# Gated cross-attention over 16 batches: score products in two 64-row halves of TensorE, and all orders written anew

## The reference

```python
# layer 0: full cross-attention, then a mixture of 8 experts (top 2)
x = x + tanh(g_xattn[0]) * attn0(layernorm(x), ctx)     # softmax(q k^T / sqrt(8)) v, 16 heads of 8
x = x + tanh(g_ffn[0])   * moe(layernorm(x))            # gelu(x W1 + b1) W2 + b2, top-2 router
# layer 1: cross-attention over the 32 greatest scores of each row, then self-attention + experts
scores = einsum('bhqd,bhkd->bhqk', q, k) / sqrt(8)
top_scores, top_idx = top_k(scores, 32)                 # of 1601
x = x + tanh(g_xattn[1]) * (softmax(top_scores) @ v[top_idx]) @ Wo.T
x = x + tanh(g_ffn[1])   * (self_attention(layernorm(x)) + top2_experts(layernorm(x)))
```

## Time and profile before

| | us |
|---|---|
| median of three runs | 5451.87 |
| the profiled execution, time | 5462.37 |
| the profiled execution, first to last instruction | 5460.3 |
| PE busy | 4684.1 (86%) |
| VectorE (DVE) busy | 4361.7 (80%) |
| ScalarE (ACT) busy | 4036.6 (74%) |
| GpSimd (POOL) busy | 1154.4 (21%) |
| mean granted TensorE clock | 0.936 of full |

### The profile page before, as it was taken

How to read it: one execution, slowest core, us unless ns; L and a number is a source line. 1 busy time by engine, 2 the same in 40 slices (tenths; PEclk the granted TensorE clock), 3 DMA queues, 4 the chain that set the end, 5 groups by cost and what they waited for, 6 DMA issues and landing times. The chain is left out here.

```text
span 5460.3 us, 110204 instructions
## 1 busy us (share of the span) xinstructions
PE 4684.1 (86%) x34502; PEld 2229.0 (41%) x34502; DVE 4361.7 (80%) x23240; ACT 4036.6 (74%) x5196; POOL 1154.4 (21%) x2648
## 2 busy tenths in 40 slices
PE   4878788999798889979989999997999799988776
PEld 2434334353343435334343544434353344434222
DVE  4458888878878797897879888788878888887772
ACT  1457677878687697868869788886878688787763
POOL 2121122222122222212212222222222122121110
PEclk7889899999899899989989999998999899999886
DMA  4232222223122132322313222231323223121110
GB/s 119 69 73 54 59 62 54 70 59 80 49 62 72 43 80 57 76 54 62 75 38 80 55 73 71 62 74 47 74 60 77 52 60 71 36 65 30 34 26 19
DMA packets 356337, 332.23 MB, mean 61 GB/s; under 512 B 102074, under 2 KB 313149, under 8 KB 355711
## 3 DMA queue, kind: packets, MB, share of 16 engines
q1 hardware_dynamic: 355710, 324.84, 24.3%
HBM read 217.54 MB, written 107.13 MB: 59 GB/s over the span
## 5 line engine op out<-in xcount | busy, mean ns | idle before, releaser
L942 DVE MAX8 cand<-s 128x8 f32<-128x67 f32 (+1 forms) x12288 | 1988.3, 222 | 116.8 <-ACT s L894 67.5
L913 ACT ACTIVATE prob<-wide 128x1024 f32<-128x1024 f32 (+1 forms) x1792 | 1778.7, 1025 | 390.2 <-PE wide L635 188.8
L1028 DVE TENSOR_REDUCE part<-score 128x1 f32<-128x512 f32 (+1 forms) x2048 | 1122.3, 564 | 395.4 <-PE score L594 264.1
L681 PE MATMUL att<-prob,v 128*9 128x256 f32 (+1 forms) x14336 | 1110.3, 389 | 27.9 <-ACT prob L913 26.1
L635 PE MATMUL wide<-q,k_att 128*128 128x256 bf16 (+1 forms) x6656 | 1023.4, 281 | 103.9 <-ACT s L894 56.2
L894 ACT ACTIVATE s<-wide 128x1024 f32<-128x1024 f32 (+1 forms) x1024 | 843.1, 845 | 309.6 <-DVEq L1082 174.5
L903 ACT ACTIVATE below<-wide 128x1024 bf16<-128x1024 f32 (+1 forms) x832 | 828.2, 1024 | 131.6 <-PE wide L635 123.5
L594 PE MATMUL score<-k_scan,q 128*128 128x512 bf16 (+1 forms) x2048 | 666.3, 349 | 220.9 <-DVE part L1028 178.7
L635 PEld LDWEIGHTS wide<-q,k_att 128*128 128x128 bf16 (+1 forms) x6656 | 583.3, 101 | 562.5 <-ACT s L894 149.5
L1271 POOL TENSOR_SCALAR flag<-cand,ends 128x24 bf16<-128x24 f32 x512 | 178.6, 349 | 2494.4 <-DVE ends L967 2243.5
L657 PE MATMUL wide<-below,minus_ident 128*128 128x512 bf16 (+1 forms) x1664 | 504.5, 386 | 97.2 <-ACT below L903 86.2
(11 more groups left out here) (161 smaller groups left out, 5202.2 us busy)
## 6 DMA issues: line engine op xcount, KB each, us to landing
k_scan<-k_stack SPq DMA_DIRECT2D x512, 150.1 KB, 2.6
k_stack<-split_b SPq DMA_DIRECT2D x576, 128.0 KB, 2.4
k_att<-k_stack SPq DMA_DIRECT2D x384, 192.0 KB, 3.3
ctxT<-in_ctx_dram SPq DMA_DIRECT2D x32, 800.5 KB, 5.2
q_stack<-split_b SPq DMA_DIRECT2D x192, 64.0 KB, 2.1
q<-q_stack SPq DMA_DIRECT2D x128, 96.0 KB
self_stack<-split_b SPq DMA_DIRECT2D x192, 64.0 KB, 2.1
k_self<-self_stack SPq DMA_DIRECT2D x64, 96.0 KB
```

The lines of the kernel that those rows point to most:

```text
L681: r = tensor.matmul(att[32 * j:32 * j + HD + 1, 0:S], v[0:kc, c, j0 * HG + j, :], m.prob[n % 3][0:kc, j * S:(j + 1) * S], start=(c == 0), ...
L913: scalar.activation(pr[0:kc, :], ps[0:kc, :], ACT.Exp, scale=SCALE).then_inc(sem["wide_done"], 1)
L942: i = vector.max(cand[:, :, c], s[:, KCUT[c]:KCUT[c + 1]])
L1028: vector.tensor_reduce(m.part[:, QT * hh + qt, c:c + 1], score[i % 2][:, 0:wd], AX.X, ALU.max).then_inc(sem["score_max"], 1)
```

## The change

1. The operands of the scores lie in two halves of the partitions, rows 0 to 50 and rows 64 to 114 (`UP = 64`). A product reads only one half (`tile_position=(r0, 0)`, 64 rows), and two products that follow each other read different halves and write different PSUM banks: in `n0` and `c1` two blocks of 512 keys of a head, in `s_0`, `s_1` and `s_z` two heads of the group, in `z_score` two heads.
2. `n0` now fills two banks at once, and `n0_max` takes one maximum over up to 1024 columns (1024 and 577). The two `score` banks are one buffer: PE may fill it only when the last maximum is done. `z_max` likewise covers two heads.
3. Operands are brought in for both halves: `q` twice (the same rows), `k_att` and the self-attention's in two halves, `k_scan` in three transfers (two for the upper half, one for the lower).
4. `ORDER` and `LAG` of all engines are written anew.

```diff
+UP = 64
+HALF = HG // 2
 ORDER = dict(
     pe="""
-        cut_add c1 pv.1 n0 c1 pv.1 c1 row_turn.0 c1 s_1 n0 s_1 n0 cut_add n0 cut_add w_k.1 pv.1 s_1*2 pv.1 n0*2
+        cut_add row_turn.0 cut_add s_1 pv.1 n0 s_1 pv.1 cut_add*2 flag s_1 pv.1 n0 s_1 pv.1 cut_add*2 c1 pv.1 n0 c1
...
 LAG = dict(
     pe={
-        "cut_add": 216, "c1": 244, "pv.1": 217, "n0": 255, "row_turn.0": 9, "s_1": 215, "w_k.1": 9, "flag": 62,
+        "cut_add": 217, "row_turn.0": 9, "s_1": 215, "pv.1": 217, "n0": 127, "flag": 61, "c1": 236, "row_turn.1": 16,
...
-        m.k_scan = [[sb(f"k_scan{l}_{n}", [P, NK], BF16) for n in range(2)] for l in range(2)]
-        m.k_att = [sb(f"k_att{n}", [P, HG, KB * P], BF16) for n in range(3)]
+        m.k_scan = [[sb(f"k_scan{l}_{n}", [P, 2, BANK], BF16) for n in range(2)] for l in range(2)]
+        m.k_att = [sb(f"k_att{n}", [P, HALF, KB * P], BF16) for n in range(3)]
-        score = [psum(f"score{n}", BANK) for n in range(2)]
+        score = psum("score", 2 * BANK)
...
                     elif name == "n0":
-                        if i >= 2:
-                            q.wait_ge(sem["score_max"], i - 1)
-                        qt, c = divmod(n, 4)
-                        a0, wd = c * BANK, min(BANK, NK - c * BANK)
-                        tensor.matmul(score[i % 2][:, 0:wd], m.q[0][g % QBUF[0]][:, hh, qt * P:(qt + 1) * P],
-                                      m.k_scan[0][(HG * g + hh) % 2][:, a0:a0 + wd],
-                                      start=True, stop=True).then_inc(sem["score_full"], 1)
+                        if i:
+                            q.wait_ge(sem["score_max"], i)
+                        for x in (1, 0):
+                            r0, wd = UP * x, min(BANK, NK - (2 * c + x) * BANK)
+                            r = tensor.matmul(score[:, x * BANK:x * BANK + wd],
+                                              m.q[0][g % QBUF[0]][r0:r0 + UP, hh, qt * P:(qt + 1) * P],
+                                              m.k_scan[0][kn % 2][r0:r0 + UP, c, 0:wd], start=True, stop=True,
+                                              tile_position=(r0, 0))
+                        r.then_inc(sem["score_full"], 1)
...
                     elif name in ("s_0", "s_1"):
-                        for j in range(HG):
-                            r = tensor.matmul(ps[0:kc, j * S:(j + 1) * S], m.k_att[kn % 3][:, j, c0:c0 + kc],
-                                              rows[:, j, :], start=(j % 2 == 0), stop=(l == 0),
-                                              skip_group_check=True)
+                        for h in range(HALF):
+                            for x in range(2):
+                                j, r0 = HALF * x + h, UP * x
+                                r = tensor.matmul(ps[0:kc, j * S:(j + 1) * S], m.k_att[kn % 3][r0:r0 + UP, h, c0:c0 + kc],
+                                                  rows[r0:r0 + UP, j, :], start=(h == 0), stop=(l == 0),
+                                                  tile_position=(r0, 0), skip_group_check=True)
...
                     elif name == "n0_max":
-                        wd = min(BANK, NK - c * BANK)
-                        vector.tensor_reduce(m.part[:, QT * hh + qt, c:c + 1], score[i % 2][:, 0:wd], AX.X,
+                        wd = min(2 * BANK, NK - c * 2 * BANK)
+                        vector.tensor_reduce(m.part[:, QT * hh + qt, c:c + 1], score[:, 0:wd], AX.X,
                                              ALU.max).then_inc(sem["score_max"], 1)
...
                     elif name == "k_scan":
-                        sync.dma_start(m.k_scan[l][kn % 2][0:ROWS, :], d.k_stack[l][b, :, :, kn % H, :]
-                                       .rearrange("n j s -> (n j) s")).then_inc(k_scan_in[l][kn % 2], 16)
+                        for c in range(2):
+                            a0 = 2 * c * BANK
+                            wd = min(BANK, NK - a0 - BANK)
+                            sync.dma_start(k_scan[UP:UP + ROWS, c, 0:wd],
+                                           stack[:, a0 + BANK:a0 + BANK + wd]).then_inc(k_scan_in[l][kn % 2], 16)
+                        sync.dma_start(k_scan[0:ROWS, :, :], stack[:, 0:3 * BANK].rearrange("p (c s) -> p c s", s=BANK)
+                                       [:, 0:3:2, :]).then_inc(k_scan_in[l][kn % 2], 16)
```

More of the change, by code:

```diff
@@ L91 @@
-        v_w2 s_0 n0*2 w_k.0 pv.0 s_0 c1 v_w2 s_0 c1 pv.0*2 n0 s_0 pv.0 s_0 n0 z_score v_w1*2 pv.0*2 flag n0 z_score
-        s_0 v_w2 w_q n0 s_0 pv.0 s_z v_w2 s_z c1 pv.0 z_score n0 s_1*2 pv_z*2 cut_add u_turn.0 cut_add z_score n0 c1
-        pv.1 w_v.0 s_1 pv.1 s_1 u_turn.2 cut_add n0*2 cut_add row_turn.2 n0 c1 pv.1 n0 c1 pv.1 s_1 ln_turn.u s_1 n0*2
-        cut_add row_turn.0 n0 cut_add z_score c1 pv.1 w_k.0 c1 pv.1 n0 s_1 z_score s_1 flag cut_add n0 cut_add z_score
-        u_q pv.1 c1 s_1 pv.1 n0 z_score s_1 cut_add n0*2 row_turn.2 cut_add c1 pv.1 n0 w_v.0 s_1 pv.1 s_1 n0*2
@@ new lines @@
+        cut_add z_score cut_add c1 pv.1 row_turn.2 c1 n0 pv.1 c1*2 ln_turn.w n0 s_1*2 cut_add n0 cut_add s_1 pv.1 n0
+        s_1 pv.1 cut_add*2 w_k.0 n0 s_1 ln_turn.v s_1 pv.1*2 row_turn.0 cut_add n0 cut_add route.v v_w1*2 flag n0
+        pv.1*2 c1 v_w2 c1*2 n0 c1 v_w2 s_1 v_w1 row_turn.1 cut_add n0 flag z_score v_w1 pv.1 c1 v_w2 c1*2 n0 w_v.0 c1
+        u_turn.1 z_score v_w1 v_w2 w_k.0 v_w1 v_w2 s_z v_w1 v_w2 s_z pv_z n0 v_w1 v_w2 w_q pv_z w_v.0 flag s_0 n0 s_0
+        v_w2 c1*2 n0 pv.0 u_turn.2 c1 pv.0 c1 n0 row_turn.2 s_0*3 pv.0 n0 s_0 pv.0 w_k.0 z_score s_0 pv.0 s_0 pv.0 s_0
@@ new lines @@
+        pv.0 s_0 ln_turn.u pv.0 s_0 pv.0 s_0 flag pv.0 u_q pv.0 s_0 pv.0 c1 s_1 pv.0 s_1 n0 cut_add u_turn.0 cut_add
+        z_score c1 pv.1 s_1 pv.1 s_1 row_turn.2 n0 cut_add*2 n0 c1 pv.1 c1 pv.1 s_1 n0 s_1 flag cut_add n0 cut_add
+        row_turn.0 c1 pv.1 c1 pv.1 n0 s_1*2 cut_add n0 cut_add c1 pv.1 n0 s_1 row_turn.1 pv.1 s_1 cut_add n0 cut_add
+        c1 pv.1 w_v.0 s_1 n0 pv.1 s_1 flag cut_add*2 n0 c1 pv.1 c1 pv.1 s_1 s_z n0 cut_add s_z pv.1 c1 n0 w_k.0 pv_z*2
+        u_turn.1 c1 w_v.0 z_score s_z*2 u_turn.2 pv_z s_0 flag pv_z s_0*2 pv.0 s_0 pv.0 u_turn.2 c1 pv.0 c1 pv.0 c1*2
@@ new lines @@
+        z_score s_0*3 pv.0 s_0 pv.0 s_0 pv.0 s_0 pv.0 flag s_0 pv.0 s_0 n0 pv.0 c1 row_turn.2 pv.0 c1 n0 pv.0 c1*2 n0
+        s_0 s_1 n0 s_1 pv.0 cut_add*2 u_turn.0 n0 s_1 pv.1 s_1 pv.1 cut_add n0 cut_add s_1 pv.1 s_1 n0 pv.1 cut_add*2
+        flag n0 s_1 pv.1 s_1 pv.1 row_turn.0 cut_add n0 cut_add c1 pv.1 n0 c1 pv.1 c1 s_1 n0 s_1 cut_add row_turn.1
+        cut_add c1 pv.1 n0 w_k.1 pv.1 s_1*2 n0 cut_add*2 s_1 pv.1 flag s_z pv.1 n0 cut_add c1 pv.1 c1 s_z n0 pv_z
+        u_turn.1 c1 pv_z c1 w_k.1 u_turn.2 w_k.1 s_0 n0 s_0*2 pv.0 s_0 n0 pv.0 s_0 pv.0 s_0 pv.0 s_0 pv.0 n0 s_0 flag
@@ L252, in streams @@
     for name in ("n0", "n0_max"):
-        of(name, name, [(g, hh, n) for g in groups for hh in range(HG) for n in range(8)])
+        of(name, name, [(g, hh, n) for g in groups for hh in range(HG) for n in range(4)])
     for name in ("c1", "c1_out"):
@@ L262, in streams @@
     for name in ("z_score", "z_max"):
-        of(name, name, [(g, h) for g in groups for h in range(HG)])
+        of(name, name, [(g, h) for g in groups for h in range(HALF)])
     for name in ("s_z", "exp_z", "pv_z"):
```

261 lines of the change are left out of this document (127 added, 134 removed), and 7 rows, old and new, of the table sp.

## The result

The changed kernel takes 5467.7 us against 5449.15 for before: ratio 1.0031 (95% interval 1.0016 to 1.0046), slower, since the interval leaves out 1. One of the 20 runs of the changed kernel is left out of the ratio: it took 11811.83 us at full granted clock, which nothing on record explains; the others lie between 5439 and 5495. The forecast was 5180 us, with 4990 to 5400 as its range; both the sign and the size were wrong.

A forecast was written before the change was run, and what follows sets the result against it. PE was taken as first of three nearly equal limits (259, 257, 252 us a batch). Summed needs fell from 768 to 728: 16 us a batch, 256 in all, giving 5196; LAG's 15 made it 5180 us, range 4990 to 5400.

The forecast's parts named there:

- PE, the products: Score products on PE (s_0, s_1, s_z, n0, c1, z_score): paired half-row products overlap fully, together 603 us less.
- PE, the changes of configuration: Switches of PE's array between tilings: 1211 more at 0.09 us each, 109 us back.
- PE's saving of 494 us: PE over the whole run: 603 us less for products minus 109 for configuration changes; 259 a batch becomes 228.
- the clock gives it back: Rival: PE's freed time lowers the granted clock to 0.91 in every batch, 5340 us; 17% with other partial returns.
- From work to time: Step from engine needs to batch time: 301 us becomes 285, 16 us a batch, 256 for 16 batches.
- the sum of the three needs: Batch time scales with PE, VectorE and ScalarE needs added up: 301 x 728/768 = 285 us.
- the 150 us of VectorE: Wider maxima on VectorE: 132 us less in n0_max and 18 in z_max; 257 a batch becomes 248.
- The one score buffer: PE filling both score banks only after the last maximum: taken as 0, between a small gain and the hand-off rival's price.
- The view named for it: Sign for the score buffer: PE's wait for a maximum under 300 us if right, for L1029 over 500 if wrong.
- score hand-off: Rival: PE stands 0.6 us at each of 1152 score-buffer fills, 14 us a batch more, 5676 us; 7%.
- `LAG` and the orders: New LAG starts c1 and rank a tenth of a round earlier: 15 us less.
- SyncE and the DMA engines: 1984 more transfers, 615 us to issue, covered by SyncE's waits; DMA share stays under 0.4: taken at 0.

The follow-up runs named there:

- e14: The kernel before with every bias product read over all 128 rows, the added rows zeros: 5311.38 us, 0.9740 of before.
- e1: The kernel before with paired half-row products in s_0, s_1, s_z, c1; n0 and z_score halved but unpaired; old orders, two score banks: 5383.98 us, 0.9873 of before.
- e6: The kernel before with each score product reading rows 0 to 63 only, one after the other: 6181.27 us, 1.1338 of before.
- e11: e1 with the first pair of products of each s_0 and s_1 issued twice, same result: 5427.97 us, 0.9974 of before.
- e7: The changed kernel with n0 maxima over 64 columns only: 5405.87 us, 0.9917 of the changed kernel.
- e15: The changed kernel with every bias product read over all 128 rows, the added rows zeros: 5255.26 us, 0.9645 of before.
- e5: The changed kernel with the orders of before, each second n0, n0_max, z_score and z_max dropped: 5423.69 us, 0.9957 of before.
- e13: e1 with every bias product read over all 128 rows, the added rows zeros: 5240.37 us, 0.9610 of before.
- e16: e5 with every bias product read over all 128 rows: 5320.25 us, 0.9753 of before.
- e3: The kernel before with the new orders, one score buffer and wide maxima, score products over all rows, unpaired: 5671.12 us, 1.0400 of before.

## Why the prediction was wrong

**"PE, the products" (-603 us): right.** Pairs overlap, and a step costs 0.23 us (0.32 less the change of 0.09), a little under the 0.25 assumed.

**"PE, the changes of configuration" (+109 us): right in number and price, not what decided.** The trace has 1211 more, and 0.09 us is what e14's gaps give at full clock. But the changes around the bias products of before were counted into the need and not looked at as something to take away, and the third gap, inside a bias product, was not seen: reading them over all rows is worth 141 us there, twice what the halves gain (e1: 66).

**The clock: the step that failed first.** The sum gave PE's saving of 494 us at full clock. The rival "the clock gives it back" took 160 us off the gain and left 112 (5340 us). The trace has a low time of 1366 us for 699, and by the estimate above 280 of the 494 us of PE are gone by that. e6 shows a lower clock where the same products read half of the rows at the same spacing, e11 a higher one where the array works more. The rival was the right mechanism with too small a price. Its clock of 0.91 is what the stretch from 800 to 4900 us was granted (0.96 before). But it rested on PE's busy share alone, and it left both ends as they were, where the clock fell from 0.81 to 0.75 and from 0.83 to 0.72. What falls into the low stretches pays most: `z_moe` took 0.70 us an instruction in before and 0.94 in the changed kernel.

**"From work to time": failed too.** Nor does a saving turn into time as the sum of the three needs has it. The 232 us by which PE's busy time did fall came back whole as idle time of PE, in waits for ScalarE (319 to 565 us). e7 took 743 us of VectorE away for 62 us of time; by the sum a microsecond of it is worth as much as one of PE's. So the 150 us of VectorE (measured on L1029 and L1045: 1139 + 175 became 1003.5 + 155, sized right) bring an estimated 12 us at e7's rate, not the 56 that the sum gives them (9 of the 40 us of need saved in a batch). The way to this sum mixed two measures, too: the 93% of PE is its busy share, with the way to PSUM in it, and its need of 259 us has none of that. Without the one-row products the change is worth 1.0% (e15 against e14: 0.9645 / 0.9740 = 0.990) where 5% was forecast.

**"The one score buffer" (0): wrong.** It costs 0.8 points from e1 to e5 and 1.4 from e13 to e16, 46 to 78 us, with the pairing of `n0` in it. The view named for it did not show this: PE's weight loads stand 245 us for a maximum, 239 before, and 416 in e1, which has two banks and is faster, and its products behind them 184, 179 and 268. The rival "score hand-off" had the sign and a price of 224 us.

**`LAG` and the orders (-15): wrong as the kernel stands,** +40 us; right in sign, and larger (-60 us), once the bias products are full-height.

**SyncE and the DMA engines (0): agreed.** e1 issues these transfers and is faster; in the changed kernel the longest sum that PE waits for one kind of transfer is 17 us (`q`, once). Not tested by itself.

Open stays how the remaining low time of e13 and e15 (1112 and 1103 us, 616 in e14) splits between fewer rows, shorter work and waits, what the one buffer and the orders cost by (e3 has them at 4 points without any halves), and why a one-row product costs 0.10 us also behind one of its own kind.

## What to carry over

A saving on TensorE is to be priced at the clock that the lighter work will be granted, and not at the clock of before: here an estimated 280 of 494 us went back. What is left counts only where the other engines do not hold TensorE up: here it all became idle time. Look in the trace for small products whose shape differs from their neighbours', and pad them with rows of zeros to the full array: 480 bias products so changed gave 2.6%, twice what the halves gave, with the same results. (Over 32 rows the padding gave nothing.) The best version is e13, halves with the old orders, two score banks and full-height bias products: 5240 us, 3.9% under before. When a change carries an order dealt anew, run it with the old order first: the order's worth changed sign with an edit elsewhere.
